# Self-attention over an image on one core: theta and phi projected with packed weight remainders, and the mix in f32

## The chip, the cores and the metric

One core of one Trainium2 chip runs the whole kernel. The time is microseconds of the device for one execution, as the median of several; lower is better. A profiled execution has a time of its own, and a span (first to last instruction) inside it.

## The reference

x is 16 images of 32 x 32 pixels x 256 channels in f32. For each image:

```python
theta = einsum('bhwc,cd->bhwd', x, W_theta)          # 32 columns
phi = maxpool2x2(einsum('bhwc,cd->bhwd', x, W_phi))  # 32 columns, 256 cells
g = maxpool2x2(einsum('bhwc,cd->bhwd', x, W_g))      # 128 columns, 256 cells
beta = softmax(einsum('bqd,bkd->bqk', theta, phi))   # 1024 pixels x 256 cells
out = gamma * (einsum('bqk,bkv->bqv', beta, g) @ W_o) + x
```

## The kernel before

TensorE multiplies `float32r` operands in one pass, with fewer bits than f32. The kernel gets its accuracy by splitting each f32 operand into a rounded high part (`_hi`, a cast) and the remainder (`_lo`, one subtraction), and adding up three products: hi x hi, hi x lo, lo x hi.

Per image i there are two halves h of 512 pixels, and these stages:

- x_high (ScalarE, line 387) and x_low (GpSimd, 499) split x, which is loaded transposed. 
- theta_phi (TensorE, 199) projects with 128 columns of weights that hold W_theta three times and W_phi once: 6 products of 512 columns into bank proj[h]. theta comes out three times because the scores use one product of depth 96 over the stack theta_hi, theta_lo, theta_hi against phi_hi, phi_hi, phi_lo. theta_high (ScalarE, 397) casts all 96 rows, theta_low (VectorE, 555) overwrites rows 32 to 63 with the remainder.
- phi_pool (VectorE, 548), phi_high (ScalarE, 402, two copies) and phi_low (VectorE, 561) make the stack of phi.
- values (TensorE, 208) projects g, again 6 products; g_pool (VectorE) pools it; g_high (ScalarE, 407) and g_low (GpSimd, 509) split it; mix (TensorE, 241) multiplies it by gamma * W_o, 6 products of 256 columns, whose result G is split by G_high and G_low.
- scores(i, n), n from 0 to 3 (TensorE, 214): two products of 256 columns each into one of two banks; maxima(i, n) (VectorE, 573) takes the negative maximum of each pixel. turn_max transposes all maxima, neg_high (ScalarE) and neg_low (VectorE) split them, and two transfers write them as two more rows under theta (`neg_in`).
- shifted(i, n) (TensorE, 261) makes scores minus maxima for 128 cells by 512 pixels; exps (ScalarE, 426) takes the exponential twice, rounded (e_hi) and full (e_sb); e_low (GpSimd, 504) subtracts.
- output(i, t), t from 0 to 7 (TensorE, 276): 6 products of 258 columns, whose last columns are the sums of the softmax. reciprocal and finish (VectorE) divide and add x.

Each engine runs its list in the order in which it is written, and waits for semaphores. The images are staggered: step s works on a = s (projections), b = s - 1 (scores, maxima, first shifts) and d = s - 2 (last shifts, outputs). The order of one step, on TensorE and on VectorE:

```python
for h in range(2):
    theta_phi(a, h); scores(b, h); shifted(d, 2 + h)
for h in range(2):
    values(a, h); scores(b, 2 + h)
outputs(d, (0, 1, 2)); turn_max(b); outputs(d, (3, 4)); mix(a); output(d, 5)
shifted(b, 0); shifted(b, 1); outputs(d, (6, 7))
```

```python
for h in range(2):
    phi_pool(a, h); theta_low(a, h); maxima(b, h)
phi_low(a)
for h in range(2):
    g_pool(a, h); maxima(b, 2 + h)
finishes(d, (0, 1)); neg_low(b); finishes(d, (2, 3, 4, 5)); G_low(a); finishes(d, (6, 7))
```

Steps 3 to 14 are alike; images 0 and 1, step 2, and what follows step 15 are written out. Loads, stores and the transfer of neg_lo are issued from SyncE's queue, that of neg_hi from ScalarE's.

Of the kernel before, what the change touches and what calls it, by code (L numbers as in the profile page):

```python
# [19 lines left out]
PROJ = P + DV  # L20
# [3 lines left out]
def nonlocal_block(nc, xt, xn, w_proj, w_out, out):  # L24
# [7 lines left out]
    with ctx:  # L32
# [57 lines left out]
        w_hi_ready, w_lo_ready = sem("w_hi_ready"), sem("w_lo_ready")  # L90
        wog_ready, wo_hi_ready, wo_lo_ready = sem("wog_ready"), sem("wo_hi_ready"), sem("wo_lo_ready")
# [5 lines left out]
        g_pooled, g_hi_ready, g_lo_ready = sem("g_pooled"), sem("g_hi_ready"), sem("g_lo_ready")  # L97
# [25 lines left out]
        def _(sp):  # L123
# [53 lines left out]
        def _(pe):  # L177
            def first_project():
                for n, c in ((0, 0), (1, 0), (0, 1), (1, 1), (2, 0), (2, 1)):
                    if n == 0:  # L180
                        pe.wait_ge(x0_hi_ready, c + 1)
                        pe.wait_ge(w_hi_ready, 1)
                    elif n == 1:
                        pe.wait_ge(w_lo_ready, 1)
                    else:
                        pe.wait_ge(x0_lo_ready, c + 1)
                    w, x = ((w_hi, x_hi), (w_lo, x_hi), (w_hi, x_lo))[n]
                    last = nc.tensor.matmul(proj[0][:, :], w[:, c, 0:P], x[:, 0, 0, c, :],  # L188
                                            start=(n == 0 and c == 0), stop=(n == 2 and c == 1))
                last.then_inc(tp_ready, 1)  # L190

            def project(i, h, cols, bank_, done):
                for c in range(CC):
                    for n, (w, x) in enumerate(((w_hi, x_hi), (w_lo, x_hi), (w_hi, x_lo))):
                        last = nc.tensor.matmul(bank_[:, :], w[:, c, cols:cols + P], x[:, i % 2, h, c, :],  # L195
                                                start=(c == 0 and n == 0), stop=(c == CC - 1 and n == 2))
                last.then_inc(done, 1)

            def theta_phi(i, h):
                if i == 1:  # L200
                    pe.wait_ge(theta_lo_ready, h + 1)
                    pe.wait_ge(phi_pooled, h + 1)
                elif i > 1:
                    pe.wait_ge(g_pooled, 2 * (i - 1) + h + 1)
                pe.wait_ge(x_lo_ready, 2 * i + h + 1)
                project(i, h, 0, proj[h], tp_ready)

            def values(i, h):
                if i > 0:
                    pe.wait_ge(theta_lo_ready, 2 * i + h + 1)  # L210
                    pe.wait_ge(phi_pooled, 2 * i + h + 1)
# [507 lines left out]
```

## Time and profile before

| what | value |
|---|---|
| median of 3 runs | 248.03 us (247.55 to 249.0) |
| profiled execution | 248.0 us, its span 246.2 us |
| TensorE (PE) busy | 235.7 us, 96% |
| VectorE (DVE) | 205.8 us, 84% |
| GpSimd (POOL) | 168.7 us, 69% |
| ScalarE (ACT) | 148.1 us, 60% |
| DMA | 208 GB/s on average |

Instructions of one engine overlap at their ends, so the distance between two starts is the price of one in a dense stretch, and the duration is how long the next engine waits for its result. The granted clock of TensorE shows 9 tenths or more in all 40 slices.

### The profile page before, as it was taken

To read this page: it belongs to the slowest core of one execution; us is meant where nothing else is said; L and a number is where in the kernel's file an instruction comes from. 1 tells how busy PE (TensorE), PEld (TensorE's weight loads), DVE (VectorE), ACT (ScalarE), POOL (GpSimd) and SP (SyncE) were. 2 spreads that over 40 slices of the span, in tenths; PEclk is the share of its full clock that TensorE was granted. 3 is DMA by queue.
4 is the path that set the end of the run, shared out by engine and by line. 5 is a ranking of instruction groups with operands and counts; after the bars stand their busy time and mean duration, and the time that the engine had idled before them with its cause. 6 is when DMAs were issued, how large, how long until landed. Compare 5 with 4: busy or idle time off the path is not lost.

```text
span 246.2 us, 4332 instructions
## 1 busy us (share of the span) xinstructions
PE 235.7 (96%) x1464; PEld 210.4 (85%) x1464; DVE 205.8 (84%) x473; ACT 148.1 (60%) x275; POOL 168.7 (69%) x119
## 2 busy tenths in 40 slices
PE   7896999999999999999999999999999999999884
PEld 4675888898989889898989989898998989899774
DVE  4587896988989898898989899898989989898855
ACT  3763865847475684847567484747749474735260
POOL 1596588676868677686958767695876779544480
PEclk9999999999999999999999999999999999999999
DMA  6790009549194775919377592928668391906924
GB/s 221 285 393 18 3 1 313 204 104 386 49 311 177 234 284 124 384 63 337 123 209 303 142 365 77 347 101 270 243 218 296 95 357 70 329 14 226 372 88 173
DMA packets 15078, 51.14 MB, mean 208 GB/s; under 512 B 1872, under 2 KB 2512, under 8 KB 15056
## 3 DMA queue, kind: packets, MB, share of 16 engines
q1 hardware_dynamic: 14368, 50.14, 58.2%
q10 hardware_dynamic: 688, 0.72, 0.8%
q8 instruction: 12, 0.20, 0.3%
q14 instruction: 10, 0.08, 0.1%
HBM read 33.95 MB, written 16.78 MB: 206 GB/s over the span
## 4 chain that ended last, share of the span: by engine, by line
PE 80%; DVE 7%; DMA 4%; ACT 3%; POOL 3%; issue 1%; ACTq 0%; DVEq 0%
PE proj L195 30%; PE out L299 24%; PE shift L299 8%; PE shift L272 6%; PE score L229 5%; PE score L256 4%; DVE neg_parts L577 3%; DMA x_t<-in_xt 2%; POOL e_lo L506 2%; DMA theta<-neg_lo 2%; PE shift L195 1%; DVE out L552 1%; DVE theta L558 1%; POOL x_lo L501 1%; PE proj L188 1%
## 5 line engine op out<-in xcount | busy, mean ns | idle before, releaser
L506 POOL TENSOR_TENSOR e_lo<-e_sb,e_hi 128x512 fp32r<-128x512 f32 x64 | 82.0, 1295 | 50.8 <-ACT e_sb L434 50.8
L501 POOL TENSOR_TENSOR x_lo<-x_t,x_hi 128x1024 fp32r<-128x1024 f32 x31 | 74.3, 2398 | 13.7 <-ACT x_hi L391 13.7
L299 PE MATMUL out<-G_hi,e_lo 128*128 128x258 f32 x188 | 53.2, 283 | 0.5 <-POOL e_lo L506 0.5
L299 PE MATMUL out<-G_hi,e_hi 128*128 128x258 f32 x188 | 53.4, 284 | 0.0
L299 PE MATMUL out<-G_lo,e_hi 128*128 128x258 f32 x188 | 53.3, 283 | 0.0
L603 DVE SCALAR_TENSOR_TENSOR y_sb<-out,r_sum,x_n 128x256 f32<-128x256 f32 x94 | 45.5, 484 | 6.4
L195 PE MATMUL proj<-x_hi,w_hi 128*128 128x512 f32 x122 | 48.4, 396 | 2.3 <-DVE theta L558 2.3
L195 PE MATMUL proj<-x_hi,w_lo 128*128 128x512 f32 x122 | 48.3, 396 | 0.0
L195 PE MATMUL proj<-x_lo,w_hi 128*128 128x512 f32 x122 | 48.2, 395 | 0.0
L431 ACT ACTIVATE e_hi<-shift 128x512 fp32r<-128x512 f32 x64 | 38.5, 601 | 13.5 <-PE shift L272 13.5
L577 DVE TENSOR_REDUCE neg_parts<-score 128x2 f32<-128x512 f32 x64 | 43.6, 685 | 1.3 <-PE score L229 0.4
L434 ACT ACTIVATE e_sb<-shift 128x512 f32<-128x512 f32 x64 | 38.5, 602 | 0.0
L299 PEld LDWEIGHTS out<-G_lo,e_hi 128*128 128x128 f32 x188 | 35.7, 190 | 0.7
L299 PEld LDWEIGHTS out<-G_hi,e_lo 128*128 128x128 f32 x188 | 35.6, 189 | 0.7 <-POOL e_lo L506 0.7
L299 PEld LDWEIGHTS out<-G_hi,e_hi 128*128 128x128 f32 x188 | 35.6, 189 | 0.7
L552 DVE TENSOR_REDUCE out<-proj 32x128 f32<-32x512 f32 x32 | 22.9, 716 | 12.3 <-PE proj L195 10.6
L391 ACT CAST x_hi<-x_t 128x1024 fp32r<-128x1024 f32 x31 | 31.2, 1050 | 0.3
L399 ACT CAST theta<-proj 96x512 fp32r<-96x512 f32 x32 | 18.7, 585 | 20.4 <-PE proj L195 19.6
L229 PEld LDWEIGHTS score<-phi,theta 96*128 96x128 f32 x128 | 23.6, 189 | 5.2
L195 PEld LDWEIGHTS proj<-x_hi,w_hi 128*128 128x128 f32 x122 | 23.0, 188 | 5.7 <-DVE theta L558 2.7
L195 PEld LDWEIGHTS proj<-x_lo,w_hi 128*128 128x128 f32 x122 | 22.9, 188 | 5.3
L195 PEld LDWEIGHTS proj<-x_hi,w_lo 128*128 128x128 f32 x122 | 23.0, 189 | 4.1
(81 smaller groups left out, 386.3 us busy)
## 6 DMA issues: line engine op xcount, KB each, us to landing
x_n<-in_xn SPq DMA_DIRECT2D x32, 512.0 KB, 7.3
x_t<-in_xt SPq DMA_DIRECT2D x31, 512.0 KB, 5.3
out<-y_sb SPq DMA_DIRECT2D x31, 512.0 KB, 6.6
x_t<-in_xt ACTq DMA_DIRECT2D x2, 256.0 KB, 4.7
w_sb<-in_w_proj SPq DMA_DIRECT2D x1, 256.0 KB, 3.7
theta<-neg_hi ACTq DMA_DIRECT2D x16, 4.0 KB
theta<-neg_lo SPq DMA_DIRECT2D x16, 4.0 KB
out<-y_sb SPq DMA_DIRECT2D x1, 256.0 KB, 2.4
```

Of the source, the lines that this page charges most:

```text
L195: last = nc.tensor.matmul(bank_[:, :], w[:, c, cols:cols + P], x[:, i % 2, h, c, :], start=(c == 0 and n == 0), stop=(c == CC - 1 and n == 2))
L229: last = nc.tensor.matmul(score[n % 2][:, NK * k:NK * (k + 1)], theta[0:THETA, i % 3, P * t:P * (t + 1)], phi[0:THETA, i % 3, :], start=(k ...
L299: last = nc.tensor.matmul(out_bank(i, t)[:, 0:GW], e[:, i % 2, KC * h + k, cells], G[:, i % 3, k, :], start=(n == 0), stop=(n == 3 * KC - 1))
L391: nc.scalar.copy(x_hi[:, i % 2, h], x_t[:, i % 2, h]).then_inc(x_hi_ready, 1)
L399: nc.scalar.copy(theta[0:THETA, i % 3, HALF * h:HALF * (h + 1)], proj[h][0:THETA, :]).then_inc(theta_hi_ready, 1)
L431: nc.scalar.activation(e_hi[:, i % 2, n, :], shift[n % 2][:, :], ACT.Exp)
L434: nc.scalar.activation(e_sb[:, n, :], shift[n % 2][:, :], ACT.Exp).then_inc(e_ready, 1)
L501: nc.gpsimd.tensor_tensor(x_lo[:, i % 2, h], x_t[:, i % 2, h], x_hi[:, i % 2, h].bitcast(f32), ALU.subtract).then_inc(x_lo_ready, 1)
L506: nc.gpsimd.tensor_tensor(e_lo[:, i % 2, n, :], e_sb[:, n, :], e_hi[:, i % 2, n, :].bitcast(f32), ALU.subtract).then_inc(e_lo_ready, 1)
L552: v.tensor_reduce(phi_max[:, P * h:P * (h + 1)], proj[h][THETA:P, :].rearrange("p (w n) -> p n w", w=WIN), AX.X, ALU.max).then_inc(phi_poo ...
L577: v.tensor_reduce(neg_parts[:, 2 * n:2 * n + 2], score[n % 2][:, :].rearrange("p (t k) -> p t k", t=2), AX.X, ALU.max, negate=True).then_i ...
L603: v.scalar_tensor_tensor(y_sb[:, h, w, :], out_bank(i, t)[:, 0:C], r_sum[:, t:t + 1], x_n[:, i % 2, h, w, :], ALU.mult, ALU.add).then_inc( ...
```

## The change

- The weights are laid in one array `w_all`: the high parts of W_theta and W_phi (64 columns), their remainders (64 columns), then high part and remainder of W_g. theta_phi becomes `pair`: two products of all 128 columns with x_hi give w_hi x_hi in rows 0 to 63 and w_lo x_hi in rows 64 to 127 of the bank; two products of 64 columns add w_hi x_lo to rows 0 to 63. 4 products in place of 6.
- copy_corr (ScalarE) copies rows 64 to 127 into SBUF, and add_corr (VectorE) adds them to rows 0 to 63 into `pair_sum` in SBUF. phi_pool and theta_high read pair_sum.
- theta exists once. theta_high casts 32 rows; theta_low is one instruction of 32 x 1024 on GpSimd; the third copy of the stack is a new transfer (`twin`) from theta's rows 0 to 31 to rows 64 to 95, on SyncE's queue. scores(i, 0) waits for both.
- mix multiplies g_max and w_og in f32, 2 products; g_high, g_low and the split of W_o go.
- In a step scores(b, h) now stand ahead of pair(a, h). At the start all loads go on SyncE's queue, x's first quarter first, and the x_low of image 0 is all on VectorE.

```diff
+            def twin(i):
+                sp.wait_ge(theta_hi_ready, 2 * i + 2)
+                sp.dma_start(theta[2 * DK:THETA, i % 3, :].bitcast(f32),
+                             theta[0:DK, i % 3, :].bitcast(f32)).then_inc(theta_twin[i % 3], 16)
...
+            def pair(i, h):
...
+                for c in range(CC):
...
+                    last = nc.tensor.matmul(proj[h][:, :], w_all[:, c, 0:P], x_hi[:, i % 2, h, c, :],
+                                            start=(c == 0), stop=(c == CC - 1), skip_group_check=True)
+                last.then_inc(corr_ready, 1)
+                for c in range(CC):
...
+                    last = nc.tensor.matmul(proj[h][0:PAIR, :], w_all[:, c, 0:PAIR], x_lo[:, i % 2, h, c, :],
+                                            start=False, stop=(c == CC - 1), skip_group_check=True)
+                last.then_inc(pair_ready, 1)
...
                 if n == 0:
-                    pe.wait_ge(theta_lo_ready, 2 * i + 2)
+                    pe.wait_ge(theta_twin[i % 3], twins(i))
+                    pe.wait_ge(theta_lo_ready, i + 1)
...
+                pe.wait_ge(g_pooled, 2 * i + 2)
                 for k in range(KC):
-                    cells = slice(P * k, P * (k + 1))
-                    for g, w in ((g_hi, wo_hi), (g_hi, wo_lo), (g_lo, wo_hi)):
-                        last = nc.tensor.matmul(mix_bank(i)[:, C * k:C * (k + 1)], g[:, cells], w[:, :],
-                                                start=(n == 0), stop=(n % 3 == 2), skip_group_check=True)
-                        n += 1
+                    last = nc.tensor.matmul(mix_bank(i)[:, C * k:C * (k + 1)], g_max[:, P * k:P * (k + 1)], w_og[:, :],
+                                            start=(k == 0), stop=True, skip_group_check=True)
...
                     for h in range(2):
-                        theta_phi(a, h)
                         scores(b, h)
+                        pair(a, h)
                         shifted(d, 2 + h)
...
+            def copy_corr(i, h):
+                act.wait_ge(corr_ready, 2 * i + h + 1)
+                if i > 0:
+                    act.wait_ge(tp_ready, 2 * (i - 1) + h + 1)
+                nc.scalar.copy(corr[:, h, :], proj[h][PAIR:P, :]).then_inc(corr_copied, 1)
...
+            def theta_low(i):
+                pool.wait_ge(theta_hi_ready, 2 * i + 2)
+                nc.gpsimd.tensor_tensor(theta[DK:2 * DK, i % 3, :].rearrange("p (h n) -> p h n", h=2), pair_sum[0:DK],
+                                        theta[0:DK, i % 3, :].bitcast(f32).rearrange("p (h n) -> p h n", h=2),
+                                        ALU.subtract).then_inc(theta_lo_ready, 1)
+                pool.wait_ge(theta_lo_ready, i + 1)
...
+            def add_corr(i, h):
+                dve.wait_ge(pair_ready, 2 * i + h + 1)
+                dve.wait_ge(corr_copied, 2 * i + h + 1)
+                if i > 0:
+                    dve.wait_ge(theta_lo_ready, i)
+                v.tensor_tensor(pair_sum[:, h, :], proj[h][0:PAIR, :], corr[:, h, :], ALU.add).then_inc(tp_ready, 1)
```

VectorE at the head of a step. Before (proj0 and proj1 are the two banks, out1<-proj is phi_pool, neg_parts<-score is maxima):

```order
L552 TENSOR_REDUCE out1<-proj0 32x128 [waits y_ready,tp_ready]
L558 TENSOR_TENSOR theta<-proj0,theta 32x512 [waits theta_hi_ready]
L577 TENSOR_REDUCE neg_parts<-score0 128x2 [waits neg_turned,score_ready]
L552 TENSOR_REDUCE out1<-proj1 32x128 [waits tp_ready]
L558 TENSOR_TENSOR theta<-proj1,theta 32x512 [waits theta_hi_ready]
L577 TENSOR_REDUCE neg_parts<-score1 128x2 [waits score_ready]
L563 TENSOR_TENSOR phi<-out1,phi 32x256 [waits phi_hi_ready]
```

The same place with the change:

```order
L590 TENSOR_REDUCE neg_parts<-score0 128x2 [waits neg_turned,score_ready]
L565 TENSOR_TENSOR pair_sum<-proj0,corr 64x512 [waits theta_lo_ready,corr_copied,pair_ready]
L565 TENSOR_TENSOR pair_sum<-proj1,corr 64x512 [waits theta_lo_ready,corr_copied,pair_ready]
L571 TENSOR_REDUCE out1<-pair_sum 32x128 [waits y_ready,tp_ready]
L571 TENSOR_REDUCE out1<-pair_sum 32x128 [waits tp_ready]
L590 TENSOR_REDUCE neg_parts<-score1 128x2 [waits score_ready]
```

Both sums (L565) now stand together, ahead of both pools, and each waits for ScalarE's copy.

ScalarE at the head of a step, with the change (corr<-proj is copy_corr, L441 and L444 are one exps):

```order
L416 COPY corr<-proj0 64x512 [waits tp_ready,corr_ready]
L441 ACTIVATE e_hi<-shift0 128x512 [waits out_ready,shifted_ready]
L444 ACTIVATE e_sb<-shift0 128x512 [waits e_lo_ready]
L416 COPY corr<-proj1 64x512 [waits tp_ready,corr_ready]
L441 ACTIVATE e_hi<-shift1 128x512 [waits out_ready,shifted_ready]
L444 ACTIVATE e_sb<-shift1 128x512 [waits e_lo_ready]
L409 CAST theta<-pair_sum 32x512 [waits tp_ready] x2
L420 CAST phi<-out1 32x256 [waits phi_pooled]
```

Before, a theta_high (96 x 512) stood ahead of each exps, and nothing behind exps but the phi copies; now a copy stands on each side of exps(d, 2), and both theta_high behind exps(d, 3).

GpSimd at the start, with the change:

```order
L513 TENSOR_TENSOR x_lo<-x_t,x_hi 128x1024 [waits x0_lo_ready,x_hi_ready]
L523 TENSOR_TENSOR theta<-pair_sum,theta 32x1024 [waits theta_hi_ready,x_lo_ready]
L513 TENSOR_TENSOR x_lo<-x_t,x_hi 128x1024 [waits x_hi_ready,theta_lo_ready]
L513 TENSOR_TENSOR x_lo<-x_t,x_hi 128x1024 [waits x_hi_ready]
L523 TENSOR_TENSOR theta<-pair_sum,theta 32x1024 [waits theta_hi_ready,x_lo_ready]
L513 TENSOR_TENSOR x_lo<-x_t,x_hi 128x1024 [waits x_hi_ready,theta_lo_ready]
```

Before, the x_lo instructions followed each other here; theta_low of images 0 and 1 now stands between them.

## Rows read from the trace of the kernel before

**Rows 1.** The page, part 1: busy us, share of the span, instructions.
```profile
PE 235.7 (96%) x1464; PEld 210.4 (85%) x1464; DVE 205.8 (84%) x473; ACT 148.1 (60%) x275; POOL 168.7 (69%) x119
```

**Rows 2.** Windows: length, busy us (instructions) per engine, PEclk, DMA share, GB/s.
```profile
110.48:124.73 14.25, 14.25 (x93) 12.90 (x93) 12.69 (x30) 9.17 (x18) 10.62 (x7) 1.00 0.64 220
```

**Rows 3.** Timeline of TensorE, one step: start us, us, engine, line, operation.
```profile
126.03 0.39 PE L195 MATMUL proj<-x_hi,w_hi 128*128 128x512 f32 x1
...
127.42 0.40 PE L229 MATMUL score<-phi,theta 96*128 96x256 f32 x2
127.66 0.39 PE L272 MATMUL shift<-theta,phi 98*128 98x512 f32 x1
...
138.24 0.73 PE L272 MATMUL shift<-theta,phi 98*128 98x512 f32 x2
...
140.26 0.39 PE L195 MATMUL proj<-x_hi,w_hi 128*128 128x512 f32 x1
```

**Rows 4.** Timeline of VectorE in the same step.
```profile
129.80 0.72 DVE L552 TENSOR_REDUCE out<-proj 32x128 f32<-32x512 f32 x1
130.55 0.68 DVE L558 TENSOR_TENSOR theta<-proj,theta 32x512 fp32r<-32x512 f32 x1
131.26 0.69 DVE L577 TENSOR_REDUCE neg_parts<-score 128x2 f32<-128x512 f32 x1
131.98 0.43 DVE L563 TENSOR_TENSOR phi<-out,phi 32x256 fp32r<-32x256 f32 x1
...
135.73 0.48 DVE L603 SCALAR_TENSOR_TENSOR y_sb<-out,r_sum,x_n 128x256 f32<-128x256 f32 x1
136.13 0.27 DVE L584 TENSOR_TENSOR neg_lo<-score,neg_hi 8x128 fp32r<-8x128 f32 x1
```

**Rows 5.** Timeline of ScalarE in the same step.
```profile
127.62 0.59 ACT L399 CAST theta<-proj 96x512 fp32r<-96x512 f32 x1 [1.01 <-PE proj L195]
128.10 0.59 ACT L431 ACTIVATE e_hi<-shift 128x512 fp32r<-128x512 f32 x1
128.59 0.59 ACT L434 ACTIVATE e_sb<-shift 128x512 f32<-128x512 f32 x1
...
131.07 0.37 ACT L404 CAST phi<-out 32x256 fp32r<-32x256 f32 x1
131.45 0.37 ACT L405 CAST phi<-out 32x256 fp32r<-32x256 f32 x1
```

**Rows 6.** Chain of waits: start us, us, what; two stretches of it.
```profile
121.12 0.11 PE score L239
...
122.67 0.72 PE score L256 x6
...
221.77 1.76 DMA theta<-neg_lo
```

**Rows 7.** The page, part 5: GpSimd's two costliest groups.
```profile
L506 POOL TENSOR_TENSOR e_lo<-e_sb,e_hi 128x512 fp32r<-128x512 f32 x64 | 82.0, 1295 | 50.8 <-ACT e_sb L434 50.8
L501 POOL TENSOR_TENSOR x_lo<-x_t,x_hi 128x1024 fp32r<-128x1024 f32 x31 | 74.3, 2398 | 13.7 <-ACT x_hi L391 13.7
```

**Rows 8.** Timeline at the start: TensorE, VectorE, and SyncE's queue.
```profile
15.51 0.64 PE L229 MATMUL score<-phi,theta 96*128 96x256 f32 x4
...
26.50 0.39 PE L195 MATMUL proj<-x_hi,w_hi 128*128 128x512 f32 x1
...
40.61 0.39 PE L195 MATMUL proj<-x_hi,w_hi 128*128 128x512 f32 x1
...
15.95 1.29 DVE L577 TENSOR_REDUCE neg_parts<-score 128x2 f32<-128x512 f32 x2 [0.36 <-PE score L229]
...
11.16 0.91 SPq L132 DMA_DIRECT2D x_n<-in_xn  x2
```

**Rows 9.** Windows of 1 us, columns as in rows 2.
```profile
13.00:14.00 1.00, 1.00 (x6) 0.82 (x5) 0.97 (x2) 0.83 (x2) 1.00 (x2) 1.00 1.04 422
...
118.80:119.80 1.00, 1.00 (x11) 1.00 (x10) 1.00 (x3) 0.81 (x1) 1.00 (x1) 1.00 0.05 21
```

More of the change, by code:

```diff
@@ L177, in _ @@
         def _(pe):
[L178 to L202, printed above, removed]
+            def pair(i, h):
+                if i == 0 and h == 0:
+                    pe.wait_ge(w_pair_lo_ready, 1)
+                elif i == 1:
+                    pe.wait_ge(tp_ready, h + 1)
@@ L211, in values @@
-                    pe.wait_ge(phi_pooled, 2 * i + h + 1)
-                project(i, h, P, value_bank(i, h), g_ready)
+                    pe.wait_ge(tp_ready, 2 * i + h + 1)
+                elif h == 0:
+                    pe.wait_ge(w_g_lo_ready, 1)
+                for c in range(CC):
+                    for n, (w, x) in enumerate(((VHI, x_hi), (VLO, x_hi), (VHI, x_lo))):
+                        last = nc.tensor.matmul(value_bank(i, h)[:, :], w_all[:, c, w:w + DV], x[:, i % 2, h, c, :],
+                                                start=(c == 0 and n == 0), stop=(c == CC - 1 and n == 2))
@@ L434, in exps @@
                 nc.scalar.activation(e_sb[:, n, :], shift[n % 2][:, :], ACT.Exp).then_inc(e_ready, 1)
-            for c in range(CC):
-                act.dma_start(x_t[:, 0, 0, c, :], xt[0, 0, :, c, :]).then_inc(x0_in[c], 16)
             first_x_high(0)
             first_x_high(1)
+            copy_corr(0, 0)
             x_high(0, 1)
-            act.wait_ge(wog_ready, 1)
-            nc.scalar.copy(wo_hi[:, :], w_og[:, :]).then_inc(wo_hi_ready, 1)
+            x_high(1, 0)
             theta_high(0, 0)
-            x_high(1, 0)
+            copy_corr(0, 1)
             x_high(1, 1)
@@ L447, in _ @@
             phi_high(0)
+            copy_corr(1, 0)
             theta_high(1, 0)
-            g_high(0)
+            copy_corr(1, 1)
             x_high(2, 0)
@@ L452, in _ @@
             x_high(2, 1)
+            neg_high(0)
             phi_high(1)
-            neg_high(0)
             G_high(0)
-            g_high(1)
-            theta_high(2, 0)
+            copy_corr(2, 0)
             exps(0, 0)
             exps(0, 1)
+            theta_high(2, 0)
+            copy_corr(2, 1)
+            G_high(1)
             theta_high(2, 1)
-            G_high(1)
+            exps(0, 2)
             phi_high(2)
-            exps(0, 2)
             exps(0, 3)
@@ L468, in _ @@
                 if s > 2:
-                    for h in range(2):
-                        theta_high(a, h)
-                        exps(d, 2 + h)
+                    copy_corr(a, 0)
+                    exps(d, 2)
+                    copy_corr(a, 1)
+                    exps(d, 3)
+                    theta_high(a, 0)
+                    theta_high(a, 1)
                     phi_high(a)
@@ L531, in _ @@
                 e_low(d, 3)
+                pool.wait_ge(e_lo_ready, 4 * d + 4)
+                theta_low(a)
                 if a < LAST:
                     x_low(a + 1, 0)
-                g_low(a)
-                if a < LAST:
                     x_low(a + 1, 1)
@@ L662, in _ @@
                 if s > 2:
-                    for h in range(2):
-                        phi_pool(a, h)
-                        theta_low(a, h)
-                        maxima(b, h)
+                    maxima(b, 0)
+                    add_corr(a, 0)
+                    add_corr(a, 1)
+                    phi_pool(a, 0)
+                    phi_pool(a, 1)
+                    maxima(b, 1)
                     phi_low(a)
```

143 lines of the change are left out of this document (75 added, 68 removed).

## The prediction

> **What bounds the kernel now.** I read the page's first part first. TensorE is busy for 96% of the span [rows 1], so any product taken off it looks like time. The view of windows says the same of one step of the main loop: 14.25 us long, and TensorE busy in all of it [rows 2]. But busy matmuls overlap, so I went to the timeline of one step, from its first projection at 126.03 us (call it T) to the next step's first at 140.26, which is 14.23 us [rows 3]. TensorE's own work, priced by starts, is 24 projections of 0.232 (six take 1.39, 126.03 to 127.42), 48 output products of 0.12, the mix 0.72, four pairs of scores of 0.24, four shifts of 0.23 and the turn 0.11 [rows 3, 6]: 14.04 us. So 0.19 us per step is not TensorE's.
>
> What is it? Follow the step along the other engines. VectorE starts phi_low at 131.98, T+5.95 [rows 4]. From there its chain (pools, maxima, two finishes) comes to neg_low at 136.13, which ends at 136.40. The transfer of neg_lo takes 1.76 us in the chain of waits [rows 6], and the two shifts start at 138.24 [rows 3]: 136.40 + 0.03 + 1.76 + 0.04 is 138.23. So the shifts wait for that transfer in every step, and from them the next T is 2.02 us away. The step is 5.95 + 6.26 + 2.02 = 14.23 us. **The kernel runs on two limits that lie 0.19 us apart**: TensorE's queue, and a loop from the projections through VectorE, the transfer of the maxima and back. Time is gained only if both get shorter.
>
> **TensorE's side.** A pair takes four products in place of six: 4 x 0.232 = 0.93 us less a step (the last two write 64 rows; a product is priced by its columns, so I leave them at 0.232). The mix becomes two products of f32 operands in place of six. The trace has no such product. From below, the turn is f32 and takes 0.11 for 128 columns [rows 6], so 2 x 256 columns are 0.44. From above I take twice today's 0.72, 1.44. I take 0.72, the row of the same mix to the same precision, which is the nearest. TensorE's own work is then 14.04 - 0.93 = 13.11 us.
>
> The Trainium skill (FP8 and Floating Point Precision, TensorE Precision Notes) has full f32 in four passes through the array. By that the mix would be 2 x 4 x 0.12 = 0.96 us and TensorE's work 13.35; no run here shows it yet.
>
> **The loop's side, step by step from T, now the start of scores(b,0).** Two pools and two theta_low lay before phi_low; now there are two add_corr and two pools, so VectorE's count is even. What changes is what they wait for.
> - TensorE: scores 0.24, pair(a,0) 0.93, so shifted(d,2) starts at T+1.17.
> - ScalarE sees it 0.44 later (127.66 to 128.10 [rows 3, 5]), T+1.61. e_hi and e_sb of exps(d,2) take 0.49 each by starts [rows 5] and stand ahead of copy_corr(a,1), which starts at T+2.59 and needs 0.59, as theta_high did [rows 5]: T+3.18. Its product was ready at T+2.3; it is the exponentials that it waits for.
> - VectorE: add_corr(a,1) starts at T+3.21. Both pools stand behind it in the queue, though pool(a,0) needs nothing of it. VectorE is through with maxima(b,0) and add_corr(a,0) at T+2.1, so it idles 1.1 us.
> - add_corr 0.71 (theta_low's price, 130.55 to 131.26 [rows 4]); the first pool between 0.61 (two VectorE instructions back to back on the same rows, 15.95 us x2 [rows 8]) and 0.75 (129.80 to 130.55 [rows 4]). Both pools read and write the same rows, as those in the 0.61 do: I take 0.62. The second pool starts at T+4.54 and ends at T+5.26.
> - ScalarE's two phi copies, 0.38 + 0.37 [rows 5], then phi_low at T+6.08. Now it waits for them; before, they were ready 0.16 us early.
>
> That is 0.13 us **later** than T+5.95. Behind phi_low nothing is changed up to the shifts, so the step is 6.08 + 6.26 + 2.02 = 14.36 us. TensorE's saving goes into waits: maxima(b,3) ends at about T+9.0 and the turn waits for it 0.8 us, then the shifts wait 0.25 us for the transfer. Its path from the turn (9.1 + 0.11 + four outputs' 1.44 and 0.72 + mix + 2.02) is 13.39 + mix: a mix of up to 0.97 us is hidden behind the transfer; with 1.44 the step is 14.83. With a pool at 0.75 it is 14.47.
>
> The skill's rule (VectorE: DVE Perf Modes, Two Vector instructions with no wait between them) holds an instruction back only if an input or output starts in another quarter of the rows than the last one's. By it the second pool is not held, 14.36; held, 14.47. The trace agrees as far as it goes: neg_low on 8 rows starts 0.40 after a finish of 0.48 [rows 4].
>
> **What is hidden.** GpSimd: theta_low over 1024 elements is priced like x_lo's 2.40 [rows 7]; g_low goes; about 12.4 us of work a step, and x_lo(a+1,1) is ready at T+12.8, needed at T'+1.6; e_lo of the next image starts at T+14.0. It would bind only above about 4 us for theta_low. The new transfer is issued at T+5.1, behind loads that are over by T+7 (one step earlier T is 111.80, and from 118.8 on the bandwidth is down to 21 GB/s [rows 9]), and is needed at T'. add_corr's wait for theta_low is long met. ScalarE gains two copies and loses g_high: about 10 of 14 us. G_low ends at T+13.9, before scores(a,0) needs it at T', a cover of 0.4 us.
>
> **Start-up.** The x halves now come on one queue and the first may be 1 us earlier, but: scores(0,0) needs the transferred theta. It is issued at about 13 us behind 2.1 MB of x_t(2) and x_n(0), issued from 9.8 us; at 0.42 MB a us [rows 9] these take until about 17, so scores(0,0) runs at about 17.3 and not 15.51 [rows 8]. GpSimd puts theta_low(0), theta_low(1) (2.4 each) ahead of x_low(1,1) and x_low(2,1); neg_high(0) now stands behind x_high(2,1). Walking the queues with the same prices, x_low(2,1) ends at 29.2 and pair(2,1) starts there, 2.7 us after 26.50 [rows 8]; it is shorter by 0.47, and the turn of image 1, which ends what follows, puts step 3's T at about 43.0, not 40.61: **+2.4 us**. If the transfer passes the loads, most of it goes: bounds 0 and 4.
>
> **Sum.** The profiled execution is 248.0 us around a span of 246.2; the median of the runs is 248.03, so both agree. 13 steps (3 to 15) x 0.13 = 1.7; start-up 2.4; the tail as before. 248.0 + 4.1 = **252.1 us**. By the page's four passes the last mix, which nothing hides, would add 0.24.
>
> **Rivals.**
> 1. *The loop is shorter than I add, and TensorE's queue is the limit* (the other side). For: 14.2 of 14.2 us busy [rows 2], and the chain of waits is mostly TensorE's work. It decides if add_corr(a,1) can start near T+2.1 rather than T+3.2 (then phi_low is at T+5.0), and the whole 0.93 is kept: 248.0 - 13 x 0.93 = 235.9, with the start-up's loss 238.3. Against: the exponentials stand ahead of the copy in ScalarE's order. Chance 0.15.
> 2. *The f32 mix is dear.* At 1.44 us the step is 14.83: 252.1 + 13 x 0.47 = 258.2. For: no row of it. It decides above 0.97. Chance 0.11.
> 3. *Nothing moves*: steps of 14.23, the start-up covered: 248 to 249. For: my 0.13 is smaller than two hand-overs. Chance 0.14, and of it 0.13 within 0.5%.
> 4. *My forecast*, its own range 249.5 to 255: 0.60.
>
> 0.5% of 248 is 1.2 us, about what a measurement can tell here. Faster: rival 1, 0.15. Same: 0.13. Slower: 0.60 + 0.11 and a remnant of rival 3, 0.72. The range leaves out rival 1 and the dear half of rival 2: 247.5 to 257.
>
> **What would show it.** Right: steps of 14.3 to 14.5; TensorE's share of busy down to about 90%, idle before the turn and the shifts, released by VectorE's maxima and the transfer; VectorE idle about 1 us before add_corr, released by ScalarE's copy; phi_low near T+6.1; step 3 beginning near 43. Wrong: steps under 14.1 with TensorE dense (rival 1), or a mix over 0.97 us (rival 2); add_corr(a,1) released by TensorE rather than ScalarE would break the step on which all rests.

## The result and the profile after

The changed kernel takes 270.83 us (median of 4 runs, 270.49 to 271.64) against 248.51 beside it: a ratio of 1.090 [1.085, 1.096], **22.3 us slower** where 4.1 were forecast. Ratios, here and below, compare the mean times of the chip's fast executions. The profiled execution has a span of 269.7 us, 23.5 more than before.

The page of the changed kernel, parts 1, 4 and 5:
```profile
PE 232.7 (86%) x1368; PEld 196.2 (73%) x1368; DVE 214.2 (79%) x476; ACT 160.8 (60%) x290; POOL 191.6 (71%) x117
...
PE 35%; DVE 32%; issue 12%; ACT 10%; DMA 8%; POOL 1%; ACTq 1%; DVEq 0%; SPq 0%
...
L523 POOL TENSOR_TENSOR theta<-pair_sum,theta 32x1024 fp32r<-32x1024 f32 x16 | 37.9, 2367 | 2.4 <-ACT theta L409 1.2
...
L565 DVE TENSOR_TENSOR pair_sum<-proj,corr 64x512 f32<-64x512 f32 x32 | 21.8, 683 | 17.0 <-ACT corr L416 14.7
L571 DVE TENSOR_REDUCE out<-pair_sum 32x128 f32<-32x512 f32 x32 | 33.5, 1084 | 0.6
```
TensorE's share falls from 96% [rows 1] to 86%; a third of the chain that ended last is VectorE's. Two rows stand out: the sum idles 17.0 us in all, 14.7 of it for ScalarE's copy, and the pool of phi takes 1084 ns, where it took 720 out of a PSUM bank [rows 4].

One step, TensorE's timeline (T is 124.85, the next 140.12), to be held against [rows 3]:
```profile
124.85 0.40 PE L246 MATMUL score<-phi,theta 96*128 96x256 f32 x2
...
134.83 0.33 PE L256 MATMUL score<-ident,neg_parts 128*128 128x128 f32 x1 [0.50 <-DVE neg_parts L590]
136.44 1.02 PE L267 MATMUL score<-w_og,g_max 128*128 128x256 f32 x4
138.10 0.73 PE L282 MATMUL shift<-theta,phi 98*128 98x512 f32 x2
140.12 0.40 PE L246 MATMUL score<-phi,theta 96*128 96x256 f32 x2
```
VectorE and then ScalarE in the same step, against [rows 4, 5]:
```profile
126.43 0.68 DVE L565 TENSOR_TENSOR pair_sum<-proj,corr 64x512 f32<-64x512 f32 x1
128.23 0.68 DVE L565 TENSOR_TENSOR pair_sum<-proj,corr 64x512 f32<-64x512 f32 x1 [1.12 <-ACT corr L416]
128.95 2.07 DVE L571 TENSOR_REDUCE out<-pair_sum 32x128 f32<-32x512 f32 x2
130.92 0.67 DVE L590 TENSOR_REDUCE neg_parts<-score 128x2 f32<-128x512 f32 x1
131.83 0.43 DVE L576 TENSOR_TENSOR phi<-out,phi 32x256 fp32r<-32x256 f32 x1 [0.24 <-ACT phi L421]
```
```profile
125.75 0.58 ACT L416 COPY corr<-proj 64x512 f32<-64x512 f32 x1 [0.29 <-PE proj L209]
126.45 0.60 ACT L441 ACTIVATE e_hi<-shift 128x512 fp32r<-128x512 f32 x1
126.94 0.59 ACT L444 ACTIVATE e_sb<-shift 128x512 f32<-128x512 f32 x1
127.56 0.58 ACT L416 COPY corr<-proj 64x512 f32<-64x512 f32 x1
```
The step is 15.27 us here, and the 12 steps from 48.53 to 232.07 average 15.30 against 14.23 (one of them is 15.57, as the shifts came 0.3 us later behind neg_low). phi_low starts at T+6.98; from it to the shifts are 6.27 us and on to T' 2.02, both as before. So the loop is the limit, and only its first part grew.

Where the 23.5 us of the span lie: the chain of step 3 begins at 48.53 and not 40.61 (+7.9); 12 steps of 1.06 (+12.8); step 15 and the end (+2.8), where the last step loses 1.07 again and the last transfer of the maxima, which nothing hides, takes 4.35 us in the chain of waits and not 2.60. That transfer differs from profile to profile: 2.71 to 3.50 us in the 15 variants of the changed kernel below, and 4.00, 3.34 and 2.61 in the three variants of the kernel before (c1, c2, b1). So the 1.8 us of it are not shown to come from the change.

### The profile page after: what moved, and what is told of

Its sections match the earlier page's. It is cut to its first block, busy times and chain, and to the rows that moved or that the text cites. A ratio compares the mean times of both kernels' runs of the same rounds, so it can differ in the third digit from the quotient of the medians.

```text
span 269.7 us, 4234 instructions
## 1 busy us (share of the span) xinstructions
PE 232.7 (86%) x1368; PEld 196.2 (73%) x1368; DVE 214.2 (79%) x476; ACT 160.8 (60%) x290; POOL 191.6 (71%) x117
## 4 chain that ended last, share of the span: by engine, by line
PE 35%; DVE 32%; issue 12%; ACT 10%; DMA 8%; POOL 1%; ACTq 1%; DVEq 0%; SPq 0%
PE out L309 14%; DVE out L571 11%; DVE neg_parts L590 8%; DVE g_max L583 7%; PE shift L282 5%; DVE pair_sum L565 5%; PE shift L309 4%; DMA theta<-neg_lo 4%; PE score L267 4%; ACT corr L416 3%; PE proj L209 3%; PE proj L215 2%; DMA theta<-theta 2%; ACT phi L421 2%; DMA x_t<-in_xt 2%
## 5 line engine op out<-in xcount | busy, mean ns | idle before, releaser
L513 POOL TENSOR_TENSOR x_lo<-x_t,x_hi 128x1024 fp32r<-128x1024 f32 x30 | 70.8, 2379 | 16.4 <-DVE x_lo L645 8.9
L309 PE MATMUL out<-G_hi,e_hi 128*128 128x258 f32 x188 | 55.9, 297 | 0.0
L441 ACT ACTIVATE e_hi<-shift 128x512 fp32r<-128x512 f32 x64 | 38.5, 602 | 18.8 <-PE shift L282 16.8
L246 PE MATMUL score<-phi,theta 96*128 96x256 f32 x128 | 28.1, 306 | 18.2 <-DVE neg_parts L590 12.2
L246 PEld LDWEIGHTS score<-phi,theta 96*128 96x128 f32 x128 | 22.5, 197 | 27.6 <-DVE neg_parts L590 18.4
L523 POOL TENSOR_TENSOR theta<-pair_sum,theta 32x1024 fp32r<-32x1024 f32 x16 | 37.9, 2367 | 2.4 <-ACT theta L409 1.2
L226 PE MATMUL proj<-x_hi,w_all 128*128 128x512 f32 x120 | 38.6, 404 | 0.0
L444 ACT ACTIVATE e_sb<-shift 128x512 f32<-128x512 f32 x64 | 38.5, 602 | 0.0
L565 DVE TENSOR_TENSOR pair_sum<-proj,corr 64x512 f32<-64x512 f32 x32 | 21.8, 683 | 17.0 <-ACT corr L416 14.7
L571 DVE TENSOR_REDUCE out<-pair_sum 32x128 f32<-32x512 f32 x32 | 33.5, 1084 | 0.6
L282 PE MATMUL shift<-theta,phi 98*128 98x512 f32 x64 | 24.5, 421 | 3.7 <-DMA theta<-neg_lo 3.5
L226 PEld LDWEIGHTS proj<-x_hi,w_all 128*128 128x128 f32 x120 | 22.2, 194 | 4.2
L209 PE MATMUL proj<-x_hi,w_all 128*128 128x512 f32 x64 | 21.5, 415 | 3.6 <-DVE g_max L583 2.0
```

The costliest lines, as they stand in the source:

```text
L226: last = nc.tensor.matmul(value_bank(i, h)[:, :], w_all[:, c, w:w + DV], x[:, i % 2, h, c, :], start=(c == 0 and n == 0), stop=(c == CC - ...
L246: last = nc.tensor.matmul(score[n % 2][:, NK * k:NK * (k + 1)], theta[0:THETA, i % 3, P * t:P * (t + 1)], phi[0:THETA, i % 3, :], start=(k ...
L282: nc.tensor.matmul(shift[n % 2][:, :], phi[0:STACK, i % 3, P * k:P * (k + 1)], theta[0:STACK, i % 3, HALF * h:HALF * (h + 1)], start=True, ...
L309: last = nc.tensor.matmul(out_bank(i, t)[:, 0:GW], e[:, i % 2, KC * h + k, cells], G[:, i % 3, k, :], start=(n == 0), stop=(n == 3 * KC - 1))
L441: nc.scalar.activation(e_hi[:, i % 2, n, :], shift[n % 2][:, :], ACT.Exp)
L444: nc.scalar.activation(e_sb[:, n, :], shift[n % 2][:, :], ACT.Exp).then_inc(e_ready, 1)
```

## Experiments

Every kernel is timed beside the kernel before; ratios are to that. The step is the distance of two chain starts in the profile.

### Is TensorE a limit of the kernel before? (c1, c2)

```diff
-                    for g, w in ((g_hi, wo_hi), (g_hi, wo_lo), (g_lo, wo_hi)):
+                    for g, w in ((g_hi, wo_hi),):
```


> The kernel before with the mix cut to its two products of rounded with rounded halves (four of six products left out, so the last digits of the output are not the reference's). Theory, the loop bounds the kernel before: the mix is 0.48 us shorter per step, but it stands between the turn and the shifts, where TensorE waits for the maxima's transfer anyway, so the time stays at 248 to 249 us. Rival, TensorE's queue was the limit: 16 x 0.48 = 7.7 us less, some 241 us.

Measured 249.43 us, ratio 1.003 [0.998, 1.007], step 14.24. 0.48 us a step less on TensorE's queue gives the kernel before nothing, though it is 96% busy. That is shown for products between the turn and the shifts, not for every place on the queue.

c2 gives the kernel before the mix of the changed one (`nc.tensor.matmul(..., g_max[...], w_og[...])`, its halves gone):

> The kernel before with the f32 mix alone (no halves of the pooled values or of the output weights). Theory: the mix takes 0.93 us in place of 0.72 in a stretch where TensorE waits anyway, and VectorE loses one subtraction and ScalarE one copy that nobody waits for: 248 to 250 us, so this part of the change costs at most 1.5 us of its 22. Rival, TensorE's queue is the limit: 16 x 0.21 = 3.4 us more, 252 us.

Measured 248.43 us, 0.999 [0.996, 1.003]. The f32 mix costs nothing that can be measured, and the loss lies in the rest of the change. Of that rest, the packing and its correction are taken apart below; scores(b, h) ahead of pair(a, h), and the new order of the loads at the start, were not tried alone.

### The two parts of the step's loss (a1, a2, a3)

a1 lets the pool read neighbours in memory (they are cells of different windows, so its output is not the reference's), a2 moves the first pool between the sums, a3 puts both copies ahead of the exponentials:
```diff
-  v.tensor_reduce(phi_max[...], pair_sum[DK:PAIR, h, :].rearrange("p (w n) -> p n w", w=WIN), ...)
+  v.tensor_reduce(phi_max[...], pair_sum[DK:PAIR, h, :].rearrange("p (n w) -> p n w", w=WIN), ...)
```
```diff
                     add_corr(a, 0)
+                    phi_pool(a, 0)
                     add_corr(a, 1)
-                    phi_pool(a, 0)
                     phi_pool(a, 1)
```
```diff
                     copy_corr(a, 0)
+                    copy_corr(a, 1)
                     exps(d, 2)
-                    copy_corr(a, 1)
                     exps(d, 3)
```


> The changed kernel, but phi_pool reads four neighbours (stride 1) of pair_sum in place of four elements 128 apart, so the cells it pools are other ones and phi is not the reference's; the number of elements is the same. Theory (it is the stride of the SBUF read that makes a pool 1.08 us long, against 0.72 from PSUM): a pool takes about 0.70 us, two by starts 1.35 in place of 2.07; phi_low moves from T+6.98 to about T+6.25, the step from 15.27 to 14.55 us; with the pools of the start-up about 259 us. Rival (any SBUF source is slow for this reduction, or GpSimd's reads beside it are what slows it): a pool stays at 1.0 to 1.1 us, the step at 15.27, the time at 270.8.

> The changed kernel, with phi_pool(a,0) ahead of add_corr(a,1) on VectorE in steps 3 to 15. Theory (the step is a loop through VectorE, and the 1.12 us for which it idles ahead of add_corr(a,1) are lost because a pool that could run is queued behind): the pool fills the idle, add_corr(a,1) stays near T+3.4, phi_low moves from T+6.98 to about T+6.0, the step from 15.27 to about 14.3 us, the time to about 258 us. Rival (VectorE's amount of work, 13.06 us a step, with its hand-overs is the limit, the order does not matter): under 2 us gained. Rival (TensorE's queue is the limit): nothing gained.

> The changed kernel, with both copy_corr of a step ahead of exps(d,2) on ScalarE. Theory (add_corr(a,1) waits for a copy that stands behind two exponentials): the copy starts when its product is ready, T+2.3, add_corr(a,1) at about T+2.95 in place of T+3.38, the step 14.85 us, the time about 265 us. Rival (the copy is off the path): 270.8. Rival (the exponentials, now 0.6 us later, hold the outputs): slower than 270.8.

a1: 260.87 us, 1.047 [1.042, 1.052]. VectorE's timeline of a1 (T is 121.66), then of a2 (T is 120.80):
```profile
125.04 0.68 DVE L565 TENSOR_TENSOR pair_sum<-proj,corr 64x512 f32<-64x512 f32 x1 [1.12 <-ACT corr L416]
125.75 1.29 DVE L571 TENSOR_REDUCE out<-pair_sum 32x128 f32<-32x512 f32 x2
...
127.87 0.43 DVE L576 TENSOR_TENSOR phi<-out,phi 32x256 fp32r<-32x256 f32 x1 [0.25 <-ACT phi L421]
```
```profile
123.09 1.11 DVE L571 TENSOR_REDUCE out<-pair_sum 32x128 f32<-32x512 f32 x1
124.23 0.68 DVE L565 TENSOR_TENSOR pair_sum<-proj,corr 64x512 f32<-64x512 f32 x1
...
127.02 0.43 DVE L576 TENSOR_TENSOR phi<-out,phi 32x256 fp32r<-32x256 f32 x1 [0.40 <-ACT phi L421]
```
Two pools of neighbours take 1.29 us, with the step of 512 bytes 2.07. In a2 the first pool fills the idle 1.12 us; 261.01 us, 1.048 [1.041, 1.055], 3 us more than expected, since phi_low came at T+6.22 and not 6.0. Either gives 10 us, since either takes 0.76 off phi_low's start. a3: 268.3 us, 1.077 [1.072, 1.083], 3 us too long: add_corr(a,1) came at T+2.96 as expected, but then phi's copies were late, behind the four exponentials, which now follow each other without a gap, and theta's two copies.

What ties these kernels together is where VectorE's queue reaches neg_low, the last VectorE instruction ahead of the transfer and the shifts: in each of them the step is that place plus 4.13 to 4.16 us, so the loop is the limit in all (h3, h5 and b1 follow below). The rows are of one step each. Single steps are longer where the transfer of the maxima lands late (one of h5's takes 14.43, with neg_low at T+9.35 as ever), so that the 12 steps of h5 average 13.58.

| kernel | phi_low after T | neg_low after T | step |
|---|---|---|---|
| before | 5.95 | 10.10 | 14.23 |
| after | 6.98 | 11.12 | 15.27 |
| a1, a2 | 6.21, 6.22 | 10.36, 10.37 | 14.51, 14.52 |
| a3 | 6.75 | 10.90 | 15.05 |
| h3 | 5.78 | 9.92 | 14.08 |
| h5 | 5.77 | 9.33 | 13.48 |
| b1 | 6.57 | 10.31 | 14.44 |

### The step in memory, and a maximum that waited for GpSimd (d1, g1, p1)

d1 lets the sum write its cells window by window (`pair_sum[:, h, :].rearrange("p (n w) -> p w n", w=WIN)` as output, theta's readers with the same step):

> The changed kernel, whose sum writes its cells window by window (a step of 16 bytes between the cells that it writes), so that the pool reads neighbours; the two readers of theta's rows read with that step instead. Theory, the 512-byte step of the pool's reads is what makes it 1.08 us, and 16 bytes cost a write nothing: pools of 0.65 us as in the run with neighbours, sums still 0.68, step 14.5 us, 260 to 262 us in all. Rival, any step costs: sums of 1.1 us, or copies of theta of 1 us and GpSimd's subtraction far over 2.4 us, then 268 us or more.

275.32 us, 1.109 [1.102, 1.117]: the rival was right. Groups of d1 by line:
```profile
L566 DVE TENSOR_TENSOR pair_sum<-proj,corr 64x512 f32<-64x512 f32 x32 | 34.5, 1079 | 13.0 <-ACT corr L416 10.0 <-issue 1.5 <-PE proj L215 0.3
L409 ACT CAST theta<-pair_sum 32x512 fp32r<-32x512 f32 x32 | 34.0, 1102 | 9.3 <-DVE pair_sum L566 9.3
...
L574 DVE TENSOR_REDUCE out<-pair_sum 32x128 f32<-32x512 f32 x32 | 20.9, 693 | 0.6
```
The pool is cured (693 ns), and the price has moved: a write with a step of 16 bytes costs VectorE 1079 ns (683 without), a read with it ScalarE 1102 (609 without). The Trainium skill (Advanced Engine Details and Errata, Memory Cachelines) has SBUF in lines of 16 bytes, with a penalty where each access goes to another line; these rows agree, and on VectorE a step of 16 bytes in the sum's write adds what 512 bytes in the pool's read add: 396 and 391 ns.

g1 pools by two elementwise maxima of neighbours:
```diff
+  v.tensor_tensor(pair_sum[DK:PAIR, h, 0:2 * P], pair_sum[DK:PAIR, h, 0:2 * P], pair_sum[DK:PAIR, h, 2 * P:HALF], ALU.max)
...
+  v.tensor_tensor(phi_max..., pair_sum[DK:PAIR, :, 0:P], pair_sum[DK:PAIR, :, P:2 * P], ALU.max)
```


> The changed kernel whose loop pools phi by two elementwise maxima of neighbouring cells (256 of 512, for the first half while VectorE waits for the second copy; then 128 of 256 of both halves at once) and not by reductions with a step of 512 bytes. Theory, the loop over phi's remainder bounds the step: behind the second sum stand 0.43 + 0.43 us in place of 2.07, phi's remainder begins at the chain's start + 5.8, the step is 14.1 us and the time 255 to 257 us, less than either of the two earlier cures (261). Rival, TensorE's queue or GpSimd is the limit by then: step 14.5 us as with either of them, 260 us.

269.29 us, 1.085 [1.078, 1.093], a miss: nearly nothing gained. g1, VectorE, then GpSimd:
```profile
128.63 0.41 DVE L576 TENSOR_TENSOR pair_sum<-pair_sum 32x256 f32<-32x256 f32 x1
129.14 1.47 DVE L582 TENSOR_TENSOR out<-pair_sum 32x256 f32<-32x256 f32 x1
```
```profile
127.29 1.29 POOL L518 TENSOR_TENSOR e_lo<-e_sb,e_hi 128x512 fp32r<-128x512 f32 x1 [0.51 <-ACT e_sb L444]
129.01 1.29 POOL L518 TENSOR_TENSOR e_lo<-e_sb,e_hi 128x512 fp32r<-128x512 f32 x1 [0.43 <-ACT e_sb L444]
```
The first maximum ran in a gap of GpSimd; the second began 0.13 us after GpSimd did and ended 0.31 after it (130.61 against 130.30). p1 writes the second as a reduction, which reads one operand:

> The run with two elementwise maxima again, with the second of them written as a reduction of two cells, which reads one operand and not two. In that run the second maximum took 1.47 us for 256 cells where the first took 0.41: it began while GpSimd subtracted and ended 0.3 us behind it. Theory, an instruction of VectorE with two operands in SBUF stands until GpSimd's is done: with one operand 0.55 to 0.8 us (step of 512 bytes included), step 14.5 us, 259 to 261 us. Rival, its shape (two blocks of 128 cells, output in PSUM) is the cause: still 1.4 us, 269 us.

261.03 us, 1.048 [1.044, 1.052]. VectorE in p1, at the same place; GpSimd's e_lo of 1.29 us began at 127.71:
```profile
127.84 0.71 DVE L582 TENSOR_REDUCE out<-pair_sum 32x256 f32<-32x512 f32 x1
```
So it was the second operand, not the shape: the Trainium skill (SBUF — State Buffer, Who interferes with whom) says that a VectorE instruction with two inputs in SBUF and GpSimd's reads shut each other out, and this trace agrees. f1 (below) shows the other direction: VectorE began first, and GpSimd's x_low took 3.14 us for its usual 2.38:
```profile
26.32 1.45 DVE L565 TENSOR_TENSOR theta<-pair_sum,theta 32x1024 fp32r<-32x1024 f32 x1
26.83 3.14 POOL L513 TENSOR_TENSOR x_lo<-x_t,x_hi 128x1024 fp32r<-128x1024 f32 x1
```
Two tiles are not the only case. In e1 (below) the product of wo_sb with one number per row took 2.12 us beside a GpSimd instruction that ended at 19.23, and 0.34 in f1, where GpSimd stood idle. Why was not tested:
```profile
17.26 2.12 DVE L665 TENSOR_SCALAR w_og<-wo_sb 128x256 f32<-128x256 f32 x1
```

### The start (a4, e1, f1, f2)

The changed kernel's start: TensorE's timeline, and two windows.
```profile
20.46 1.22 PE L246 MATMUL score<-phi,theta 96*128 96x256 f32 x4 [5.96 <-DMA theta<-theta]
...
31.33 0.73 PE L209 MATMUL proj<-x_hi,w_all 128*128 128x512 f32 x2 [2.03 <-DVE g_max L583]
```
```profile
18.00:24.00 6.00, 3.54 (x12) 2.94 (x13) 2.68 (x4) 0.80 (x2) 1.19 (x1) 0.50 0.59 180
24.00:30.00 6.00, 5.31 (x19) 3.89 (x17) 3.52 (x6) 3.69 (x7) 4.60 (x2) 0.76 0.10 23
```
The first of these windows in the kernel before:
```profile
18.00:24.00 6.00, 3.74 (x20) 2.88 (x19) 4.73 (x9) 2.81 (x6) 4.32 (x2) 1.00 0.13 51
```
theta's copy is issued at 14.32 and lands 6.1 us later; TensorE has then idled for 5.96 us, it is granted 0.50 (1.2 GHz) from 18 to 24 us, and four products of scores take 1.22 us and not 0.64 [rows 8]. a4 issues the transfers of images 0 and 1 on ScalarE's queue; e1 replaces them by a copy of ScalarE; f1 has their theta_low on VectorE; f2 is e1 and f1.

> The changed kernel, with the transfer of theta's third copy of images 0 and 1 issued from ScalarE's queue, where no loads stand before it. Theory (at the start it lands 6.1 us after its issue because 2 MB of loads are ahead of it in the same queue, and the idle TensorE then runs at the lower clock until 28 us): it lands about 2.5 to 3 us after the issue, scores(0,0) at about 17.3 us in place of 20.46, less time at the lower clock, the time about 267 us. Rival (the next waits of the start, x_lo(1,1) on GpSimd until 19.2 us and neg_high behind x_high, are as late): under 1 us gained.

> The changed kernel with the second copy of theta's rounded half, of images 0 and 1 alone, written by ScalarE (two copies more of some 1 us) and not by a transfer. Theory, the start-up loses its time because TensorE stands for 6 us until the transfer lands and then has half its clock: scores of image 0 begin near 17.5 in place of 20.5, the clock stays up, the chain of step 3 begins near 45 in place of 48.5, 267 us in all. Rival, the copies and subtractions of the start on ScalarE and GpSimd are as late anyway: within 1 us of 270.8.

> The changed kernel with theta's remainder of images 0 and 1 alone on VectorE (1.2 us each) and not on GpSimd. Theory, the start-up is bound by two things at once, the transfer of theta's copy and GpSimd's three subtractions of 2.4 us in a row, so that taking away the second alone gives less than 2 us: the chain of step 3 begins at 47 to 48.5, 269 to 271 us in all. Rival, GpSimd's queue alone was the cause: 45.5, 268 us.

> The changed kernel with both: theta's remainder of images 0 and 1 on VectorE, and the second copy of its rounded half by ScalarE. Theory, two causes at once: only now does the projection of image 1 follow the first scores at once (near 18 in place of 21.5), all of step 2 comes 3 us earlier, step 3 begins near 45.5 and the time is 267 to 268 us. Rival, the start is bound by the order of ScalarE's queue and by the clock: no more than either alone, 270 us.

| kernel | us | ratio | scores(0,0) | pair(2,0) |
|---|---|---|---|---|
| after | 270.83 | 1.090 [1.085, 1.096] | 20.46 | 31.33 |
| a4 | 273.31 | 1.096 [1.091, 1.102] | 20.31 | 31.91 |
| e1 | 270.91 | 1.092 [1.085, 1.098] | 16.90 | 30.53 |
| f1 | 270.54 | 1.088 [1.082, 1.095] | 19.44 | 30.32 |
| f2 | 269.89 | 1.085 [1.080, 1.089] | 17.48 | 29.48 |

Three of four missed. Another queue doesn't help: in a4 the transfer took 6.5 us from its issue at 13.8, with no load ahead of it in its queue. (a4 is also 2.5 us longer than the changed kernel; why stays open.) In e1 TensorE ran its first scores 3.6 us earlier and then waited elsewhere:
```profile
19.38 1.19 PE L207 MATMUL proj<-x_hi,w_all 128*128 128x512 f32 x2 [1.76 <-POOL x_lo L517]
...
30.53 1.22 PE L207 MATMUL proj<-x_hi,w_all 128*128 128x512 f32 x2 [4.30 <-DVE g_max L587]
```
What pair(2,0) waits for is g_pool(1,0), behind phi_low(1), behind phi's copies, which stand behind x_high(2,1), neg_high(0) and the issue of its transfer (1.24 us) in ScalarE's order. And theta_low on VectorE, expected at 1.2 us, took 2.03 and 1.45 in f1.

### Mending the order (g2, h1, h2, h3)

g2 is g1 with f2's start, a3's order and phi's copies ahead of theta's.

> All cures together: the two elementwise maxima, both copies of the corrections ahead of the exponentials, phi's copies ahead of theta's on ScalarE, and for images 0 and 1 theta's remainder on VectorE and its second copy by ScalarE. Theory: phi's remainder begins at the chain's start + 5.4, the step is 13.7 us, step 3 begins near 45.5, 247 to 250 us in all, so that the change with its order mended is no slower than the kernel before. Rival, another engine is the late one by then (GpSimd's subtractions, since theta's remainder comes later, or TensorE): steps of 14.1 us or more and 254 us.

264.87 us, 1.063 [1.055, 1.070], a miss for g1's reason, not yet known then. h1 cures the step in memory by layout: x is laid out so that a window's cells are neighbours in the banks (three transpositions in what lays the arrays out), and both pools read `"p (n w) -> p n w"`. h2 adds the orders of a2 and a3 and phi's copies ahead of theta's; h3 adds f2's start and, for image 1, phi's copies and phi_low and g_pool ahead of the maxima's halves.

> The changed kernel with its arrays laid out so that the four cells of a window are neighbours in a bank's columns (x transposed, x natural and the output in that order), so that both pools read neighbours; the result is the reference's. Theory, the step of 512 bytes is what VectorE's pool pays for in SBUF: pools of phi of 0.65 us, step 14.5 us, 260 to 262 us, as in the run that only read neighbours. Besides, the pool of the values, which reads a PSUM bank, shows whether a step costs anything there: 0.69 us as before if not. Rival, the reordered layout itself costs (stores or loads of x in another order): above 264 us.

> As the run with the layout, and with the steady order mended: the first pool between the two sums, both copies of the corrections ahead of the exponentials, phi's copies ahead of theta's. Theory, the loop over phi's remainder bounds the step and each of the three stands on it: phi's remainder begins at the chain's start + 5.1, the step is 13.4 to 13.7 us, 246 to 250 us in all. Rival, TensorE's own queue (86% busy in the changed kernel) or GpSimd is the bound by then: steps of 14.0 us or more, 253 us.

> As the run before it, with the start mended too: theta's remainder of images 0 and 1 on VectorE, its second copy by ScalarE, and phi's copies and remainder of image 1 ahead of the turned maxima on ScalarE and VectorE. Theory, the start is bound by the order of ScalarE's and VectorE's queues and not by the transfer: the projection of image 2 begins near 26 in place of 31.3, step 3 near 43.5, and the time is 4 to 5 us below the run with the mended steady order, 242 to 245 us. Rival, what bounds the start is the clock or GpSimd: less than 2 us below it.

h1: 260.81 us, 1.045 [1.039, 1.051], as expected; g_pool, out of PSUM, takes 686 ns with neighbours, and 686 with the step in the changed kernel. h2: 254.57, 1.022 [1.017, 1.027], step 14.07. h3: 252.32, 1.013 [1.008, 1.018], step 14.08, the chain of step 3 at 43.54 (h2: 49.14). Both miss their sums: phi_low came at T+5.78, not 5.1, since phi's copies stood behind the exponentials:
```profile
120.36 0.43 DVE L582 TENSOR_TENSOR phi<-out,phi 32x256 fp32r<-32x256 f32 x1 [0.76 <-ACT phi L423]
```
The steps are now shorter than before's. h3 is 2.3 us under h2, though its start looks 5.6 earlier: among the nine kernels with the changed kernel's order of the start (after, a1, a2, a3, d1, g1, h1, h2, p1) that place lies between 46.7 and 50.5, so the median is what counts.

### What the saved products are worth (h5, b1)

```diff
+                    maxima(b, 2)
                     phi_low(a)
+                    maxima(b, 3)
                     for h in range(2):
                         g_pool(a, h)
-                        maxima(b, 2 + h)
```
h5 puts this on h3, b1 on the kernel before.

> The run with layout, steady order and start mended (252.3 us, step 14.07), with VectorE's maxima of the last two pairs of tiles ahead of its pools of the values, and the third of them ahead of phi's remainder. Theory, the loop runs through VectorE's queue behind phi's remainder (4 instructions of 0.6 us before the turn), so this takes 1.2 us or more out of it, and TensorE's own queue becomes the limit: a step of 13.4 to 13.7 us, 245 to 247.5 us in all, below the kernel before. Rival, something that stands behind the loop decides (the transfers of the maxima, GpSimd, or the projections that wait for the pools of the values): 14.0 us or more, 251 us.

> The kernel before with the same order of VectorE's maxima and nothing else. Theory, the same loop bounds it at 14.23 us and TensorE's queue at 14.04: the loop falls away and TensorE's queue decides, 14.05 us a step, 2 to 3 us less in all, 246 to 247 us. The difference to the run above is then what the change's fewer products are worth once the loop does not cover them, less its longer start. Rival: nothing moves, 249 us.

**h5: 245.11 us, 0.984 [0.979, 0.989]**, 1.6% less than the kernel before and the first to be below it, step 13.48, as expected. VectorE in h5 (T is 114.41) shows why; the page of h5, parts 1 and 4, what is left:
```profile
119.35 0.67 DVE L596 TENSOR_REDUCE neg_parts<-score 128x2 f32<-128x512 f32 x1
120.18 0.43 DVE L582 TENSOR_TENSOR phi<-out,phi 32x256 fp32r<-32x256 f32 x1 [0.17 <-ACT phi L423]
...
123.74 0.27 DVE L603 TENSOR_TENSOR neg_lo<-score,neg_hi 8x128 fp32r<-8x128 f32 x1
```
```profile
PE 227.5 (94%) x1368; PEld 197.8 (81%) x1368; DVE 208.0 (85%) x478; ACT 162.2 (67%) x292; POOL 186.7 (77%) x115
...
PE 77%; DVE 9%; DMA 6%; issue 3%; ACT 1%; POOL 1%; SPq 1%; DVEq 0%; ACTq 0%
```
The maximum now fills VectorE's idle time before phi_low (0.17 us left of 0.76), and neg_low comes 0.59 us earlier, at T+9.33: all of the step's gain. The expectation's reason was only half right: the number of instructions ahead of neg_low did not change, the idle time did. That it came to 13.48 all the same is in part luck. TensorE is at 94%, and the chain is mostly its own.

b1: 250.61 us, 1.006 [1.003, 1.010], a miss, for the same reason. The kernel before had no idle time there to fill, and the order makes one, since maxima(b,3) now comes before its scores are ready:
```profile
119.95 0.69 DVE L577 TENSOR_REDUCE neg_parts<-score 128x2 f32<-128x512 f32 x1 [0.23 <-PE score L229]
```
neg_low comes 0.2 us later than in the kernel before, the step is 0.2 longer. So with its queues put in order and its cells laid out as neighbours the packed kernel has a step 0.75 us shorter than the old one's (0.65 on the average of 12 steps, where some transfers land late); whether another order would help the old one was not tried.

## Why the prediction was wrong in its size

- **What bounds the kernel**: right. Two limits close together, and work taken off TensorE's queue worth nothing while the loop stands (c1). Rival 1 did not come.
- **The mix**: 0.72 taken. The mix takes 0.86 us in the chain of waits of the changed kernel, where six products took 0.72 [rows 6]; its two products come as four records. The prediction's estimate of 0.96, from the four passes of the Trainium skill (FP8 and Floating Point Precision, TensorE Precision Notes), was the nearer figure. Hidden, as forecast (c2).
- **add_corr(a,1) at T+3.21**: the mechanism right (idle 1.12 us for ScalarE's copy, forecast 1.1), the place T+3.38. The copy starts 0.62 us after the exponential ahead of it, where 0.49 was taken from a pair of exponentials, and the hand-over to VectorE took 0.09 and not 0.03. It is not that a copy never overlaps: theta's copy (96 rows, from row 0) stands 0.48 ahead of an exponential in the kernel before [rows 5]. The corrections are read from row 64 of the bank; phi's copies, read from row 96, also start 0.61 behind an exponential there (130.46 to 131.07). That the first row is the cause fits these rows and was not tested.
- **The failed term: the pools at 0.62 (start to start) and 0.72 (the second's duration).** They were priced by rows that read PSUM banks [rows 4, 8], while the change makes them read SBUF with a step of 512 bytes. Sum and pools took 2.79 us in place of 2.05. That term alone turns 14.36 into 15.10, and with the copy's 0.17 into 15.27, which is what was measured; it makes 9.6 us of the 18.2 that the forecast is short. a1, h1 and p1 each give it back, so it is the step in memory and not SBUF as such. (With a pool at 0.75 the prediction's step is 14.49, not 14.47.)
- **From phi_low to the shifts and T'**: 6.26 and 2.02 forecast, 6.27 and 2.02 found.
- **The start**: +2.4 forecast, bounds 0 and 4, +7.9 found in the profile. The transfer landed at 20.4 and not 17.3 (the forecast's own rows, 2.1 MB from 9.8 us at 0.42 MB a us, give 14.8 for the loads, not 17, so that sum was off before it was tested), the clock fell to half, and the queues' walk was too short: pair(2,1) ran at 33.08 and not 29.2. The clock was in no term. What is shown: without the transfer nothing is gained (e1), without GpSimd's theta_low 0.3 us, which lies within the runs' spread (f1), without both 0.9 (f2), and both with the order of image 1's copies give 2.3 (h3 against h2). The rest of the start's loss stays open.
- **The tail** "as before": 1.8 us more in the profile for the last transfer of the maxima, which takes 2.6 to 4.35 us in these profiles whatever the kernel. Not shown to be the change's.

## What to carry to other kernels

Before taking work off the busiest engine, measure what that engine is worth by leaving work out of it: here 0.48 us a step on an engine 96% busy were worth nothing. When an instruction's operand moves from PSUM to SBUF, look again at its step in memory and at how many operands lie in SBUF, before the old duration is used. And a wait put into a queue holds up what stands behind it: a pool that fits into the idle time ahead of the wait was worth 10 us.

## What the runs showed of the hardware

- A step in SBUF costs time on each of the three engines measured: VectorE's reduction 1084 ns for 693, its sum's write 1079 for 683, ScalarE's copy 1102 for 609, GpSimd's subtraction 2905 for 2367. Out of a PSUM bank a step of 512 bytes costs VectorE nothing (686 ns with and without).
- A VectorE instruction with both operands in SBUF waited for GpSimd's (1.47 us for 0.41 in g1), and GpSimd's for VectorE's when that had begun first (3.14 for 2.38 in f1).
- On ScalarE theta's copy, which reads from row 0 of the bank, starts 0.48 us ahead of an exponential (kernel before); the copy of the corrections, which reads from row 64, starts 0.62 behind one and 0.61 ahead of the next.
- A transfer of 128 KB inside SBUF took 6.1 us behind loads that had been issued before it, and a queue of its own did not make it land sooner (6.5 us, in a4).
- After 6 us of idling (14.5 to 20.46) TensorE was granted 0.50 from 18 to 24 us and 0.76 from 24 to 30; in the kernel before, where its longest wait there was 1.65 us, it had 1.00 in both.
